# Early-fusion transformer layer: the routing of the last two tiles rewritten, GpSimd's products put ahead of the table loads, a constant's load moved back

## Chip, cores and metric

The kernel runs on one core of a Trainium2 chip. The metric is the device time of one execution in microseconds (us), lower is better. A core has five engines that run on their own and wait for each other by semaphores: TensorE (PE in the profile; PEld is its weight load), VectorE (DVE), ScalarE (ACT), GpSimd (POOL) and SyncE (SP, which only issues transfers), and 16 DMA engines that all queues share.

## What is computed

Eight sequences of 164 tokens (36 patch embeddings and 128 text tokens) with 192 channels pass one attention layer and one mixture-of-experts layer:

```
xn   = layernorm(layernorm(h), ln_w)
attn = causal_softmax((xn * W_qk[h]) (xn * W_qk[h])^T / sqrt(192))      # 12 heads
out  = (attn (xn - mean(wte))) / (position + 1)                         # wte: 50257 x 192
h    = h + out W_o^T
n    = normed(layernorm(h)) * ln_w;  probs = softmax(n W_router)        # 16 experts
keep the first 64 tokens per expert and sequence; y = relu(n wi[e]) wo[e] where kept, else n
h    = h + h_normed + max(probs) * y
```

## The kernel before

**Attention, one sequence at a time** (`iteration(b)` on PE, DVE, ACT and GpSimd, b = 0 to 7; the queues' order is written out by hand). A sequence is cut in 128 rows (A) and 36 rows (B). DVE makes z (the layer-normed rows), PE transposes it, ACT copies it to `zT`. GpSimd multiplies `zT` by the heads' weights `w2` (`weigh`, L385 to 390): six products into `AwA` (three groups of four heads, two halves of the channels each) and two into `AwB`. PE's `score(b, r)` needs them: round r = 0, 1, 2 takes two products of `AwA` each, rounds 3 and 4 take `AwB`. Then DVE takes row maxima (L786, L790), ACT exponentials (L552, L557), DVE the factors `rn` (L798), GpSimd multiplies them in (`normalise`, L416: three tiles of `PA`, two of `PB`). PE transposes P (L1274 to 1280), ACT and DVE copy a high and a low part (`PTAH` L565, `PTAL` L803, `PTB` the same for B), and `value(b, g)` multiplies by the values into `bO` and `bE` (g = 3 is the B part, `PTB0`, `PTB1`); ACT and DVE copy those out (`oTA`, `oTB`, L570, L808), and `project` multiplies by `W_o` into `bJ`, which `residual` adds to `H`. The scores of sequence b + 1 are put between the steps of sequence b. In PE's order `score(b+1, 0)` follows `value(b, 2)`, and `score(b+1, 1)` and `value(b, 3)` come after it.

**The table's mean** runs beside the attention. `wte` comes in 28 chunks of 1344 KB. Two are loaded into `wbuf`'s two slots. 20 are added onto them by transfers that accumulate, issued by GpSimd (`add_wte`, L396 to 401, three in each `iteration` of b = 0 to 5, the slots in turn); each issue waits until the transfer before it in its slot has landed. Six go through one more buffer, `plain` (SP, L284 to 287): DVE sums it in four pieces per sequence (`plain_sum`, L822), and the next load is issued only after the fourth. In DVE's order `plain_sum(b, 0)` stands right in front of `row_max(b + 1, 0)`. During sequence 6 all sums are folded together and the mean is taken out of `H`.

**Routing.** The 1312 tokens lie in 11 tiles (`SLOTS`: eight A tiles, three of 96 B rows). Nine are routed in a first stage (`STAGE[0]`), the last two (A tile of sequence 7, last B tile) in a second. For a stage DVE runs `routed` (maximum, first best expert, one-hot `oh`), PE ranks (`text_rank`: `oh` against constant matrices `mat`), DVE `keep` (`kp`, rank under 64), PE `expert_rank` (counts over all tiles, into `bT`), DVE `place` (row numbers `posI` in the expert table). `row_scales` refines 1/sqrt with one Newton step, `base_factors` makes the factors with which ACT (`bases`) writes the normed rows and the base rows to `pay`. `link` makes DVE wait for each operation before the next. GpSimd then scatters tile after tile to `dispatched` (L458). When all have landed, SP loads the first block of rows, and PE starts the experts with `x_transpose(0, 16)`. From the moment the number of blocks is known until then it runs 34 matmuls on ones (`stay_warm(bJ, 34)`). 16 blocks of 112 rows follow, PE back to back.

`mat` is 1024 KB in float32 (`mat32`), loaded by SP at its queue's start, in front of the first plain load (L304), and copied to bf16 by ACT (L608) between sequences 1 and 2.

Of the kernel before, what the change touches and what calls it, by code (L numbers as in the profile page):

```python
# [58 lines left out]
def program(nc, patches, projw, projb, pos, txtA, txtB, txtBp, wqk, lnw, lnc, wte, wo_attn,  # L59
# [9 lines left out]
    with ctx:  # L69
# [88 lines left out]
        capB = sb("capB", [128, EXP])  # L158
# [122 lines left out]
        def _(sp):  # L281
# [21 lines left out]

            sp.dma_start(mat32, cst2_d[:, C_MAT:NCST2]).then_inc(mat_in, 16)  # L304
            plain_loads(sp)
# [55 lines left out]
        def _(pool):  # L361
# [118 lines left out]
            for j in range(n0, SLOTS):  # L480
                pool.wait_ge(norm_ready, j - n0 + 1)
                pool.wait_ge(base_ready, j + 1)
                scatter(j)
# [26 lines left out]
        def _(act):  # L510
# [94 lines left out]
            iteration(1)  # L605

            act.wait_ge(mat_in, 16)
            nc.scalar.activation(mat[:, :, :].rearrange("p m s -> p (m s)"), mat32, ACT.Copy).then_inc(mat_ready, 1)  # L608
            with act.Fori(2, LAST - 1) as b:
                iteration(b)  # L610

            def bases(g, k0=None, k1=None):
                act.wait_ge(basepar_ready, g + 1)
                lo, hi = GROUPS[g]
                for k in range(lo if k0 is None else k0, hi if k1 is None else k1):
                    if g == 0:
                        nc.scalar.activation(norm[:, k, :], H[:, ORD[k], :], ACT.Identity, bias=nmc[:, k:k + 1],
                                             scale=rsq[:, 1, k:k + 1]).then_inc(cen_ready, 1)
# [14 lines left out]
            def lx_exp(B):  # L633
                k0, k1 = STAGE[B]
                act.wait_ge(le_ready, 2 * B + 2)
                nc.scalar.activation(lx[:, k0:k1, :], lg[:, k0:k1, :], ACT.Exp).then_inc(lx_ready, 1)

# [999 lines left out]
```

## Time and profile before

| | us |
|---|---|
| median of 3 runs (376.38 to 377.46) | 377.38 |
| profiled execution, its own time | 378.11 |
| its span, first to last instruction | 376.3 |
| busy in the span: PE, PEld, DVE, ACT, POOL | 338.9, 308.9, 220.6, 126.1, 169.0 |
| mean granted TensorE clock | 0.962 |

The span divides roughly into set-up (to 25 us), sequences 0 to 7 (to 257), routing (to 291) and experts (to 369). The granted clock is given as a share of the full 2.4 GHz, so 0.50 is 1.2 GHz. Busy shares are means; what counts is which wait ends last at each place.

### The profile page before, as it was taken

Reading aid. Unit: us, or ns where it says so; the run is one execution under the profiler, and the core shown is the slowest. Engines: PE = TensorE matmul, PEld = TensorE weight load, DVE = VectorE, ACT = ScalarE, POOL = GpSimd, SP = SyncE. Lnnn points to the kernel's source line nnn. Section 1 sums busy time; section 2 is a strip of 40 time slices with the busy share of each in tenths; the row PEclk is TensorE's granted clock in tenths of the full one; section 3 lists DMA queues with packets and bytes.
Section 4 is the critical chain, followed back from the end, with each engine's and each line's share of the span. In section 5 each row is a group of like instructions: output and inputs, shape, how many; then the busy total and the mean of one; then the engine's idle time right before and its main releaser. Section 6 shows DMA issues by size and latency. Waiting matters only on the chain.

```text
span 376.3 us, 6812 instructions
## 1 busy us (share of the span) xinstructions
PE 338.9 (90%) x2360; PEld 308.9 (82%) x2360; DVE 220.6 (59%) x556; ACT 126.1 (34%) x433; POOL 169.0 (45%) x181
## 2 busy tenths in 40 slices
PE   5987699999899899899898998998859999999992
PEld 2866499899699799798897998997723999999991
DVE  2378638668669578587677978657485222222221
ACT  2055424644453445426345024539100111111110
POOL 3058474674663862954836203140751134433321
PEclk9699969999999999999999999999968999999997
DMA  7499999799799799898997999600222499999950
GB/s 226 151 410 332 214 207 212 203 194 213 210 200 236 198 188 271 169 195 251 174 210 187 291 209 241 148 0 2 107 95 71 108 288 276 258 250 264 270 150 17
DMA packets 20176, 74.29 MB, mean 197 GB/s; under 512 B 3388, under 2 KB 9021, under 8 KB 18874
## 3 DMA queue, kind: packets, MB, share of 16 engines
q0 software_dynamic: 7344, 30.57, 40.3%
q1 hardware_dynamic: 9898, 40.40, 36.6%
q10 hardware_dynamic: 2912, 3.04, 3.1%
q8 instruction: 12, 0.20, 0.2%
q14 instruction: 10, 0.08, 0.1%
HBM read 66.12 MB, written 9.25 MB: 200 GB/s over the span
## 4 chain that ended last, share of the span: by engine, by line
PE 44%; issue 19%; POOL 15%; DVE 9%; DMA 7%; ACT 4%; POOLq 1%; SPq 0%; DVEq 0%; ACTq 0%
PE bO L1190 19%; PE bE L1190 10%; PE bS L1190 6%; POOL AwA L390 5%; PE bJ L1190 5%; DMA wbuf<-in_wte 4%; POOL PA L416 4%; POOL wbuf L401 3%; POOL AwB L390 2%; DMA AwA<-in_patches 2%; ACT PA L552 2%; PE bT L1190 1%; DVE negmax L786 1%; POOL PB L416 1%; PE bT L1535 1%
## 5 line engine op out<-in xcount | busy, mean ns | idle before, releaser
L552 ACT ACTIVATE PA<-bS,negmax 128x128 f32<-128x128 f32 x96 | 33.9, 366 | 85.4 <-DVE negmax L786 85.4
L416 POOL TENSOR_TENSOR PA<-PA,rn 128x512 f32<-128x512 f32 x24 | 25.5, 1062 | 66.4 <-DVE rn L798 66.3
L390 POOL TENSOR_TENSOR AwA<-zT,w 96x512 f32<-96x512 f32 x45 | 53.4, 1515 | 3.3 <-ACT zT L534 3.3
L1190 PE MATMUL bJ<-wo_sb,oTA 128*128 128x192 f32 x288 | 52.1, 331 | 0.0
L1190 PEld LDWEIGHTS bS<-zT,AwA 96*128 96x128 f32 x384 | 48.4, 198 | 1.2
L1190 PE MATMUL bS<-zT,AwA 96*128 96x128 f32 x384 | 48.4, 281 | 0.0
L1190 PEld LDWEIGHTS bJ<-wo_sb,oTA 128*128 128x128 f32 x288 | 47.2, 193 | 0.0
L1190 PE MATMUL bO<-PA,wx 96*128 96x112 f32 x384 | 45.4, 275 | 0.5 <-DVE PA L1163 0.5
L1190 PEld LDWEIGHTS bO<-PA,wx 96*128 96x128 f32 x384 | 44.9, 192 | 0.7 <-DVE PA L1163 0.7
L463 POOL DMA_INDIRECT out<-PA,yrow x16 | 15.0, 940 | 58.7 <-DVE PA L1179 58.7
L683 ACT ACTIVATE AwA<-bO 128x448 f32<-128x448 f32 x16 | 8.7, 543 | 82.6 <-PE bO L1190 74.1
L1190 PE MATMUL bE<-wx,AwA 128*112 128x192 f32 x192 | 33.8, 326 | 0.0
L822 DVE TENSOR_REDUCE wx<-wx 128x672 f32 (+1 forms) x24 | 31.5, 1314 | 0.0
L1190 PEld LDWEIGHTS bE<-wx,AwA 128*112 128x112 f32 x192 | 30.4, 177 | 0.0
L401 POOL DMA_DIRECT2D wbuf<-in_wte x20 | 27.2, 1359 | 5.0 <-DMA wbuf<-in_wte 3.9
L1172 DVE TENSOR_SCALAR AwA<-bO 128x224 f32<-128x224 f32 x16 | 6.3, 392 | 36.0 <-PE bO L1190 31.8
L786 DVE TENSOR_REDUCE negmax<-bS 128x4 f32<-128x512 f32 x24 | 16.5, 687 | 14.4 <-PE bS L1190 14.3
L416 POOL TENSOR_TENSOR PB<-PB,rn 108x328 f32<-108x328 f32 x16 | 11.7, 733 | 28.1 <-DVE rn L798 27.3
L458 POOL DMA_INDIRECT dispatched<-pay,posI x11 | 12.4, 1125 | 19.3 <-ACT pay L619 13.7
L570 ACT ACTIVATE oTA<-bO,lncol 128x512 f32<-128x512 f32 x24 | 16.6, 690 | 13.1 <-PE bO L1190 13.1
L1190 PE MATMUL bS<-zT,AwB 96*108 96x164 f32 x128 | 20.3, 302 | 0.0
L1190 PE MATMUL bO<-wo_sb,oTB 128*96 128x192 f32 x108 | 18.1, 327 | 2.2 <-DVE oTB L808 1.5
(248 smaller groups left out, 697.2 us busy)
## 6 DMA issues: line engine op xcount, KB each, us to landing
wbuf<-in_wte POOLq DMA_DIRECT2D x20, 1344.0 KB, 12.9
wx<-in_wi SPq DMA_DIRECT2D x16, 576.0 KB
wx<-in_wo SPq DMA_DIRECT2D x16, 576.0 KB
wx<-in_wte SPq DMA_DIRECT2D x6, 1344.0 KB, 8.5
dispatched<-zeros SPq DMA_DIRECT2D x7, 675.5 KB, 10.6
wbuf<-in_wte SPq DMA_DIRECT2D x2, 1344.0 KB, 11.4
AwA<-dispatched ACTq DMA_DIRECT2D x14, 168.9 KB
wo_sb<-in_wo_attn SPq DMA_DIRECT2D x1, 1728.0 KB, 6.7
```

Source lines behind the costliest of these rows:

```text
L390: nc.gpsimd.tensor_tensor(o, zT[:, k, ss].unsqueeze(1).to_broadcast(list(o.shape)), w2[:, k, hs].unsqueeze(2).to_broadcast(list(o.shape)), ...
L401: pool.dma_start(wchunk[s], wv[:, ds(c, 1), :].rearrange("p c x -> p (c x)"), accum_op=ALU.add, max_dma_last_dim=WR * EMB * 4 // 2).then_i ...
L416: nc.gpsimd.tensor_tensor(t, t, q.unsqueeze(2).to_broadcast(list(t.shape)), ALU.mult).then_inc(p_ready, 1)
L458: nc.gpsimd.indirect_dma_start(out=xd[:, :], out_offset=bass.IndirectOffsetOnAxis(ap=posI[0:n, j:j + 1], axis=0), in_=pay[0:n, j, :], in_o ...
L463: nc.gpsimd.indirect_dma_start(out=out[:, :], out_offset=bass.IndirectOffsetOnAxis(ap=idx, axis=0), in_=rows, in_offset=None, bounds_check ...
L552: last = nc.scalar.activation(PA[:, h, :], bank[:, j * SA:(j + 1) * SA], ACT.Exp, bias=negmax[:, h:h + 1], accum_out=lsum[:, h:h + 1])
L570: nc.scalar.activation(dst, src, ACT.Copy, scale=lncol[:, 0:1]).then_inc(o_used, 1)
L683: nc.scalar.activation(hT[:, 0:4, :], bO[0][:, 0:4 * T].rearrange("p (c n) -> p c n", c=4), ACT.Relu).then_inc(h0_ready, 1)
L786: nc.vector.tensor_reduce(negmax[:, 4 * r:4 * r + 4], bS[r % 2][:, :].rearrange("p (h s) -> p h s", h=4), X, ALU.max, negate=True).then_in ...
L822: nc.vector.tensor_reduce(psums.rearrange("p (n e) -> p n e", e=EMB)[:, ds(b, 1), q].rearrange("p n e -> p (n e)"), plain.rearrange("p (r ...
L1172: nc.vector.tensor_scalar(hT[:, 4:6, :], bO[1][:, 0:2 * T].rearrange("p (c n) -> p c n", c=2), 0.0, None, ALU.max).then_inc(h1_ready, 1)
L1190: return nc.tensor.matmul(o, l, r, start=start, stop=stop, skip_group_check=True)
```

## The change

1. GpSimd: in every `iteration`, four `AwA` products stand in front of the first accumulating load instead of behind it, and the other two loads move behind a later step each. In sequence 0 all three `normalise` of `PA` stand in front of the first two loads.
2. SP loads `mat32` behind the six plain loads; ACT copies it to bf16 in sequence 6 instead of between sequences 1 and 2. DVE's factors for sequences 2 to 7 move into sequence 0's iteration, behind its third `e_copy`.
3. Routing: a Newton step has three operations instead of four; `kept` and one of the `drop` operations are gone (`kept` comes once, after the table of blocks); the last two tiles' normed rows come from ACT instead of DVE (L987), their exponents are scaled and summed by ACT (`slot_exp`); stage 0's `row_scales` and `base_factors` move behind `routed`; `shift` spares stage 1 an operation. PE's `expert_rank(0)` stands before `value(LAST, 3)` instead of behind it.
4. `stay_warm(bJ, 34)` becomes `stay_warm(bJ, 26)`.

```diff
-            sp.dma_start(mat32, cst2_d[:, C_MAT:NCST2]).then_inc(mat_in, 16)
             plain_loads(sp)
+            sp.dma_start(mat32, cst2_d[:, C_MAT:NCST2]).then_inc(mat_in, 16)
...
-            normalise(0, range(1))
+            normalise(0, range(3))
             add_wte(2, 0, 0)
-            normalise(0, range(1, 2))
             add_wte(3, 1, 0)
-            normalise(0, range(2, 3))
...
-                for k in range(4):
-                    if r is not None and k < 3:
-                        add_wte_nth(i, r + k)
-                    if k == 0:
-                        weigh(b + 1, t_before(b, "z") + 1, (0, 1), (0, 1))
-                    elif k == 1:
-                        weigh(b + 1, t_before(b, "z") + 1, (0, 1), (2,))
-                        normalise(b + 1, (0,))
-                    elif k == 2:
-                        normalise(b + 1, (1,))
-                        weigh(b + 1, t_before(b, "z") + 1, (0, 1), (3,))
-                    else:
-                        normalise(b + 1, (2,))
+                n = t_before(b, "z") + 1
+                weigh(b + 1, n, (0, 1), (0, 1))
+                if r is not None:
+                    add_wte_nth(i, r)
+                weigh(b + 1, n, (0, 1), (2,))
+                normalise(b + 1, (0,))
+                if r is not None:
+                    add_wte_nth(i, r + 1)
+                normalise(b + 1, (1,))
+                weigh(b + 1, n, (0, 1), (3,))
+                if r is not None:
+                    add_wte_nth(i, r + 2)
+                normalise(b + 1, (2,))
...
+            def slot_exp(k):
+                act.wait_ge(le_ready, 3)
+                act.wait_ge(basepar_ready, 1 + k - GROUPS[0][1] + 1)
+                nc.scalar.activation(lx[:, k, :], lg[:, k, :], ACT.Exp, scale=rsq[:, 1, k:k + 1],
+                                     accum_out=lsm[:, k:k + 1]).then_inc(lx_ready, 1)
...
-                link(nc.vector.tensor_tensor(t, t, x, ALU.mult))
-                link(nc.vector.tensor_scalar(t, t, -0.5, 1.5, ALU.mult, ALU.add))
-                link(nc.vector.tensor_tensor(y, y, t, ALU.mult))
+                link(nc.vector.scalar_tensor_tensor(t, t, -0.5, x, ALU.mult, ALU.mult))
+                link(nc.vector.scalar_tensor_tensor(y, t, 1.5, y, ALU.add, ALU.mult))
...
             row_factor(0, 2)
-            factors(2, NBATCH, 2)
...
                 e_copy(b, 2)
+                if is0(b):
+                    factors(2, NBATCH, 2)
                 plain_sum(b, 0)
...
-            row_scales(0)
-            base_factors(0)
...
             routed(0)
-            exponents(0)
+            row_scales(0)
+            exponents()
+            base_factors(0)
             keep(0)
-            probability(0)
+            homes(0)
             place(0)
...
             routed(1)
-            norms(2)
-            exponents(1)
+            row_scales(2)
             keep(1)
-            probability(1)
+            base_factors(2)
+            homes(1)
             place(1)
...
-            value(LAST, 3)
+            project(LAST, 12, 14)
             pe.wait_ge(t_used, TPB * NBATCH)
             pe.wait_ge(tl_used, 5 * NBATCH)
             expert_rank(0)
-            project(LAST, 12, WCH)
+            value(LAST, 3)
+            project(LAST, 14, WCH)
...
-            stay_warm(bJ, 34)
+            stay_warm(bJ, 26)
```

GpSimd, the loop's body for an even sequence, before (`wbuf<-in_wte` is an accumulating load, ISA rows are register and semaphore work):

```order
L416 TENSOR_TENSOR PB<-PB,rn 108x328
L399 ISA
L401 ISA
L401 DMA wbuf<-in_wte 128x2x1344
L385 ISA
L390 TENSOR_TENSOR AwA<-zT,w 96x512 x4
L401 ISA
L401 DMA wbuf<-in_wte 128x2x1344
L390 TENSOR_TENSOR AwA<-zT,w 96x512 x2
```

The same place of the changed kernel:

```order
L416 TENSOR_TENSOR PB<-PB,rn 108x328
L385 ISA
L390 TENSOR_TENSOR AwA<-zT,w 96x512 x4
L399 ISA
L401 ISA
L401 DMA wbuf<-in_wte 128x2x1344
L390 TENSOR_TENSOR AwA<-zT,w 96x512 x2
```

The four products no longer stand behind a load, and the second load has moved on behind `normalise(b + 1, 0)`, which is not shown; the third moved from ahead of `normalise(b + 1, 1)` to behind the two `AwB` products.

DVE in the second stage of the routing, from the one-hot to the placing's first operation, before:

```order
L1008 TENSOR_TENSOR oh<-cst,lidx 128x32
L724 TENSOR_TENSOR nwt<-rsq 128x2
L725 TENSOR_TENSOR nwt<-nwt,var 128x2
L726 TENSOR_SCALAR nwt<-nwt 128x2
L727 TENSOR_TENSOR rsq<-rsq,nwt 128x2
L978 TENSOR_SCALAR rsq<-rsq 128x1
L979 SCALAR_TENSOR_TENSOR nmb<-fmv,rsq 128x1
L987 TENSOR_SCALAR pay<-H,fmv,rsq 128x192
L1012 TENSOR_TENSOR lg<-lg,rsq 128x32
L1024 SCALAR_TENSOR_TENSOR kp<-bS,oh 128x32
L1027 TENSOR_REDUCE kept<-kp 128x2
L1028 TENSOR_SCALAR drop<-kept 128x2
```

And of the changed kernel:

```order
L1001 TENSOR_TENSOR oh<-cst,lidx 128x32
L726 TENSOR_TENSOR nwt<-rsq 128x2
L727 SCALAR_TENSOR_TENSOR nwt<-nwt,var 128x2
L728 SCALAR_TENSOR_TENSOR rsq<-nwt,rsq 128x2
L1024 SCALAR_TENSOR_TENSOR kp<-bS,oh 128x32
L978 SCALAR_TENSOR_TENSOR nmc<-fmv,rsq 128x1
L979 TENSOR_SCALAR rsq<-rsq 128x1
L980 SCALAR_TENSOR_TENSOR nmb<-fmv,rsq 128x1
L1018 TENSOR_SCALAR drop<-lidx 128x2
L1036 TENSOR_SCALAR capI<-bT 128x16
```

`kp`, which PE waits for, now follows the Newton step directly, and four operations instead of nine lie between it and the placing (before, three more followed the last row shown: `drop`, `lsm` and the reciprocal).

## Rows read from the trace of the kernel before

**Rows 1.** Timeline of PE, sequence 0: start, length, instruction [idle before <-releaser].

```profile
38.14 0.31 PE L1233 MATMUL bT<-cst,zA 128*96 128x128 f32 x1 [2.03 <-DVE PTAL L803]
...
47.58 0.59 PE L1190 MATMUL bS<-maskA,idb 128*128 128x512 bf16 x1 [2.94 <-issue]
...
56.59 0.44 PE L1190 MATMUL bO<-PTB0H,vAH 128*128 128x432 f32 x1
```

**Rows 2.** Timeline of POOL, sequence 0.

```profile
44.21 1.21 POOL L401 DMA_DIRECT2D wbuf<-in_wte  x1 [2.11 <-DMA wbuf<-in_wte]
44.97 4.49 POOL L390 TENSOR_TENSOR AwA<-zT,w 96x512 f32<-96x512 f32 x4
```

**Rows 3.** Windows: busy of PE, PEld, DVE, ACT, POOL, PEclk, DMA share, GB/s.

```profile
48.00:50.00 2.00, 2.00 (x11) 2.00 (x10) 0.00 (x0) 0.00 (x0) 1.46 (x2) 0.50 1.03 210
...
98.00:124.00 26.00, 24.27 (x175) 22.91 (x174) 19.06 (x37) 11.73 (x47) 15.91 (x16) 1.00 0.93 207
```

**Rows 4.** Timeline of DVE, sequence 0.

```profile
44.67 0.48 DVE L808 TENSOR_SCALAR oTA<-bE,lncol 128x256 f32<-128x256 f32 x1 [1.44 <-PE bE L1190]
...
51.62 0.69 DVE L786 TENSOR_REDUCE negmax<-bS 128x4 f32<-128x512 f32 x1 [5.26 <-PE bS L1190]
```

**Rows 5.** Timeline of PE, sequence 3.

```profile
102.17 0.39 PE L1190 MATMUL bS<-maskA,idb 128*128 128x512 bf16 x1 [0.92 <-POOL AwA L390]
...
108.67 0.43 PE L1190 MATMUL bO<-PTB0H,vAH 128*128 128x432 f32 x1 [0.26 <-DVE PTB1L L803]
```

**Rows 6.** Timeline of POOL, sequence 3, and the products of sequence 6.

```profile
98.76 1.21 POOL L401 DMA_DIRECT2D wbuf<-in_wte  x1
...
109.42 1.21 POOL L401 DMA_DIRECT2D wbuf<-in_wte  x1 [0.28 <-issue]
...
203.46 6.03 POOL L390 TENSOR_TENSOR AwA<-zT,w 96x512 f32<-96x512 f32 x6
```

**Rows 7.** Who waited, 60 to 200 us: total, times, longest.

```profile
PE bS L1190 <- POOL AwA L390: 4.1, 5, 0.9
...
PE bT L1233 <- DVE PTAL L803: 0.4, 1, 0.4
```

**Rows 8.** Timeline of DVE, sequences 3 and 4.

```profile
104.38 0.69 DVE L786 TENSOR_REDUCE negmax<-bS 128x4 f32<-128x512 f32 x1 [1.39 <-PE bS L1190]
...
127.94 1.31 DVE L822 TENSOR_REDUCE wx<-wx 128x672 f32 x1
```

**Rows 9.** The plain loads' line L287, 100 to 180 us: issue starts, landing.

```profile
L287 SPq DMA_DIRECT2D wx<-in_wte x3: 328/328/328, 118.2 to 170.6; - x3
...
DMA to landing us min/median/max: 8.0/8.5/8.8
```

**Rows 10.** DMA queues, 146 to 148 us: packets, MB, share of 16 engines.

```profile
q0 software_dynamic: 70, 0.33, 81.1%
q1 hardware_dynamic: 17, 0.18, 21.9%
```

**Rows 11.** Timelines of DVE and PE, first stage of routing.

```profile
259.88 0.17 DVE L1039 TENSOR_SCALAR capI<-bT 128x16 int32<-128x16 f32 x1 [1.41 <-PE bT L1190]
...
263.39 3.14 PE L1190 MATMUL bO<-wo_sb,oTB 128*96 128x192 f32 x18 [1.51 <-DVE oTB L808]
```

**Rows 12.** Timeline of DVE, second stage.

```profile
272.68 0.19 DVE L1008 TENSOR_TENSOR oh<-cst,lidx 128x32 bf16<-128x32 f32 x1
...
274.43 0.18 DVE L1024 SCALAR_TENSOR_TENSOR kp<-bS,oh 128x32 bf16<-128x32 f32 x1
...
278.87 0.16 DVE L1062 TENSOR_TENSOR posI<-drop,posF 128x2 int32<-128x2 f32 x1
```

**Rows 13.** Timelines of PE and SP before the experts.

```profile
281.15 9.88 PE L1190 MATMUL bJ<-ones 128*128 128x512 bf16 x34 [1.49 <-DVE nbI L1147]
...
285.21 1.27 SPq L238 DMA_DIRECT2D AwA<-dispatched  x3
```

**Rows 14.** Window at that place, columns as in rows 3.

```profile
288.00:289.00 1.00, 1.00 (x7) 0.46 (x5) 0.00 (x0) 0.00 (x0) 0.00 (x0) 1.00 0.17 60
```

More of the change, by code:

```diff
@@ L604, in _ @@
             iteration(0)
[L605 to L609, printed above, removed]
+            with act.Fori(1, LAST - 1) as b:
                 iteration(b)
@@ L646, in _ @@
             o_copy(b, 2)
+            act.wait_ge(mat_in, 16)
+            nc.scalar.activation(mat[:, :, :].rearrange("p m s -> p (m s)"), mat32, ACT.Copy).then_inc(mat_ready, 1)
             exps(LAST, (0,))
@@ L676, in _ @@
             nt_slot(7, 10, bO[1])
-            lx_exp(1)
+            slot_exp(9)
+            slot_exp(10)
             bases(2)
@@ L1008, in routed, with exponents, homes @@
                 nc.vector.tensor_tensor(part(oh, B), em, part(lidx, B).unsqueeze(2).to_broadcast(bc), ALU.is_equal).then_inc(oh_ready, 1)
-            def exponents(B):
-                (k0, k1), s = STAGE[B], STAGE[B][1] - STAGE[B][0]
-                nc.vector.tensor_tensor(part(lg, B), part(lg, B), rsq[:, 1, k0:k1].unsqueeze(2).to_broadcast([128, s, EXP]),
+            def exponents():
+                (k0, k1), s = STAGE[0], STAGE[0][1] - STAGE[0][0]
+                nc.vector.tensor_tensor(part(lg, 0), part(lg, 0), rsq[:, 1, k0:k1].unsqueeze(2).to_broadcast([128, s, EXP]),
                                         ALU.mult).then_inc(le_ready, 1)
             def probability(B):
-                dve.wait_ge(lx_ready, B + 1)
-                link(nc.vector.tensor_reduce(part(lsm, B), part(lx, B), X, ALU.add))
+                if B:
+                    dve.wait_ge(lx_ready, 3)
+                else:
+                    dve.wait_ge(lx_ready, 1)
+                    link(nc.vector.tensor_reduce(part(lsm, B), part(lx, B), X, ALU.add))
                 nc.vector.reciprocal(pay[:, STAGE[B][0]:STAGE[B][1], D_RP], part(lsm, B)).then_inc(rp_ready, 1)
+            def homes(B):
+                link(nc.vector.tensor_scalar(part(drop, B), part(lidx, B), float(T), float(BIG + EXP * T), ALU.mult, ALU.add))
             def keep(B):
@@ L1026, in keep @@
                 dve.wait_ge(kp_ready, B + 1)
-                link(nc.vector.tensor_reduce(part(kept, B), part(kp, B), X, ALU.add))
-                link(nc.vector.tensor_scalar(part(drop, B), part(kept, B), -float(BIG), float(BIG + EXP * T), ALU.mult, ALU.add))
-                link(nc.vector.scalar_tensor_tensor(part(drop, B), part(lidx, B), float(T), part(drop, B), ALU.mult, ALU.add))
             def place(B):
@@ L1059, in place @@
                     link(nc.vector.tensor_tensor(u, u, t, ALU.add))
-                link(nc.vector.tensor_tensor(u, u, part(kp, B), ALU.mult))
+                link(nc.vector.scalar_tensor_tensor(u, u, -float(BIG), part(kp, B), ALU.add, ALU.mult))
                 link(nc.vector.tensor_reduce(part(posF, B), u, X, ALU.add))
+                probability(B)
                 nc.vector.tensor_tensor(part(posI, B), part(drop, B), part(posF, B), ALU.add).then_inc(pos_ready, 1)
+                if not B:
+                    link(nc.vector.scalar_tensor_tensor(shift[:, :], cst2[:, C_EM:C_EM + EXP], -float(T), first[:, 0, :],
+                                                        ALU.mult, ALU.subtract))
             b = NBATCH - 2
```

45 lines of the change are left out of this document (20 added, 25 removed).

## Prediction

> **What bounds the kernel now.** I read the page's slices of busy time first, then the windows, then the list of waits, and then each engine's timeline at the places that the diff touches. In the middle sequences PE is busy 24.3 of 26 us at full clock [rows 3]. So PE's order is the bound, and only its idle pieces can be won. The list of waits between 60 and 200 us has one large one, for `AwA` from GpSimd: 4.1 us in five waits of up to 0.9 [rows 7], one per sequence, in front of `score(b+1, 0)` [rows 5]. Three places differ from this pattern. In sequence 0 PE stands 2.03 us for DVE's low part, then 2.94 us in front of `score(1, 0)` [rows 1], and then runs at half clock, 0.50 in the window at 48 us [rows 3]. In the routing a chain of small DVE operations bounds [rows 11, 12]. Before the experts PE runs matmuls whose results nobody reads [rows 13]. The experts themselves the change leaves alone. The DMA engines are the second resource to watch: their share is 0.93 between 98 and 124 us [rows 3].
>
> **Sequence 0.** (a) DVE's six linked operations for sequences 2 to 7 leave the place in front of the low parts. The wait for these is 2.03 us [rows 1]. Six operations at about 0.2 us, one of them stretched, make 1.9 us; I take 1.85, bounds 1.2 (six at 0.2) and 2.03 (the whole wait). All that follows shifts with it. (b) In front of `score(1, 0)` GpSimd waits 2.11 us for a landed load, issues one in 0.76 us (44.21 to 44.97) and only then starts the products [rows 2], while PE waits 2.94 [rows 1]. After the change the products come directly behind `normalise`, and the load's wait falls behind them. The products start then at about 40.8 us: the first two `wte` issues, now between the `PA` and `PB` tiles, cost some 0.5 of what was open. Two products take 2.0 us (six take 6.03 when no load stands among them [rows 6]), so the score starts at 42.9 instead of 47.58: 4.7 us with (a) in it. (c) The clock. From `score(1, 0)` to `value(0, 3)` the trace has 9.0 us at sequence 0 [rows 1] and 6.5 at sequence 3 [rows 5]. The difference, 2.5 us, is the half clock behind the stall. With the stall reduced to some 0.4 us I expect no drop. (d) Back comes 0.55 us: the moved factors, now five operations of 0.2, and `plain_sum(0, 0)` of 1.3 us [rows 8] stand between DVE's third copy, which ends at 45.1 [rows 4] and then at 43.25, and `row_max(1, 0)`, which starts then at 45.65 instead of 45.1. Together 4.7 + 2.5 - 0.55 = **6.65 us**, bounds 4.0 (the clock falls all the same) and 7.2.
>
> The price of this part lies on the DMA side: the first accumulating load is issued at 36.5 us, behind three `normalise`, instead of at 31.6. Each of those loads occupies the engines for 6.5 us (1344 KB at 210 GB/s [rows 3]). I followed the slots forward: GpSimd then sits behind a landing until about 59.0 us, in front of `normalise(1, 2)`, which PE wants 2 us later. I count nothing for it, up to 2 us in the range.
>
> **The loop, b = 1 to 5.** With the products in front of the load, the first two are done 2.0 us after the last `PB` tile, while PE has `value(b, 2)` to do for 2.5. So the 0.82 us mean wait falls, 4.1 us in all [rows 7]. But the loads move: the three issues, now at 0, 4.8 and 10.7 us after the last `PB` tile [rows 6], would come at 4.1 (four products), 9.7 (two more and a `normalise`) and 15.9 us (another and `AwB`). Their transfers, three times 7 us, then end at 27 us instead of 23. The plain load issued 19.5 us after that tile, at 118.2 [rows 9], now finds 5.6 us of accumulating traffic in front of it or beside it; before, it found 1. Its `plain_sum` comes 9.7 us after the issue, at 127.94 [rows 8], and it lands after 8.0 to 8.8 us [rows 9]. If both queues share the engines evenly, the plain load takes 3.3 + 3.3 us of engine time instead of 3.3 + 1.0, and lands 2.3 us later, after 10.8: 1.0 us too late. The sum stands in DVE's order directly ahead of `row_max(b+1, 0)`, which has 1.39 us of slack [rows 8], of which the earlier score takes 0.92 [rows 5]. So about 0.5 us of delay reaches `exps`, the `PTB` copies and `value(b, 3)`, which waits for these already [rows 5]. Net 0.9 - 0.5 = 0.4 us a sequence, **2.0 us**. The bounds: +4.1 if the plain load is in time, and -9.9 if it is served only when no accumulating packet is there (a landing after 13.1 us, 2.8 us of delay a sequence: 4.1 - 14).
>
> What speaks for even sharing: while the one drained and the other came, the queues had 81% and 22% of the engines in a window of 2 us [rows 10], and the window's tail, in which the plain queue has the larger part, cannot be told from draining. The Trainium skill says the same as my assumption with an open side: by "DMA: Bandwidth & Descriptors", section "Queues, rings and completion order", each engine goes round the queues and changes only at the end of a packet, which may hold many descriptors. By that rule the plain load can be kept from half of the engines' time at least, and more where the accumulating packets are the longer ones; no run here shows it yet.
>
> The constants' copy on ACT (between sequences 1 and 2) held up P's transposed tiles: PE waited 0.4 us once [rows 7]. It moves to sequence 6, where ACT stands idle for over 15 us while DVE folds the table. **0.4 us**. The transfer, 1024 KB, leaves the crowded start, which helps the first loads, and comes behind the sixth plain load; it is wanted 30 us later.
>
> **Routing, first stage.** PE now does `expert_rank(0)` before `value(LAST, 3)`. In the trace `place(0)` began at 259.88 after a wait of 1.41 us, and PE stood 1.51 us for `oTB`, the copy behind it [rows 11]. The ranks were done at 256.7; `kp` follows 0.35 later, two chunks of `project` fill that, the counts take 0.7, so `place` starts at about 258.0. It and the probability that moved into it (0.55) end 1.3 us earlier. The copy then waits for PE's `value` (ends 260.5) less than for DVE; `project_b` starts at 262.25 instead of 263.39. **1.1 us**. Below is nothing if DVE's nine operations between one-hot and `kp` do not fit into PE's last `project` (they need 1.4 us, PE gives 1.5); above is the whole wait, 1.5. ACT's eighteen rows start 2.2 us later and end at 265.1, before GpSimd needs any of them.
>
> **Second stage.** From the one-hot to `posI` the trace has 272.68 to 279.03, 6.35 us [rows 12], all of it linked DVE work. What goes: one Newton operation 0.2, the normed row on DVE 0.45, the scaling 0.1, `kept` 0.22, one `drop` 0.2, the sum of exponents 0.22, one `first` 0.2; what comes is 0.1 for a factor. **1.4 us**, bounds 1.1 and 1.6. ACT's two exponents with sums (not in the trace in this size; nearest the 128x32 one, 0.23, and the attention's 0.37 with 0.19 for the read of the sum) and its rows end 2 us before they are waited for.
>
> **The filler.** 34 matmuls take 9.88 us [rows 13]: about twelve at half clock (0.43) and 22 at full (0.214). The eight that go are of the fast kind: 1.7 us. What is late next is the first block of rows: SP issues its loads at 285.21 [rows 13], and the transfers are over in the window from 288 to 289 [rows 14]. Landed at 288.5 to 289, against a filler that would end at 289.3, they just fit. **1.7 us**, below 1.2.
>
> **Sum.** 6.65 + 2.0 + 0.4 + 1.1 + 1.4 + 1.7 = 13.25 us. Against the profiled execution's own 378.11 (1.8 over its span) that is 364.9; the median of the three runs lies 0.7 below that execution, at 377.38, so **364.1 us**.
>
> **Rivals.** Less than 0.3% (1.1 us) either way cannot be told from no change.
> - *The plain load is in time.* The accumulating tail gives way, as the plain queue's larger share at the end of that window might mean. The loop gives all its 4.1 us: 362.0. Chance 0.22.
> - *The plain load is served last* (the packet rule at its hard end). `plain_sum` holds `row_max` by 1.2 to 2.8 us a sequence: 367.5 to 375.6. Chance 0.15.
> - *GpSimd's late first loads catch up with it in sequence 1, or the clock falls in sequence 0 all the same.* 2 to 2.6 us are lost: 366.5. For it speaks that the DMA engines have only 7% of air; against it, that the slots come round every two loads. Chance 0.12.
> - *Slower.* The same place in DVE's order as the second, but with the plain load also delayed by the next sequence's accumulating load: then the delay is no longer bounded by 2.8 us. The gains outside the loop are 11.25, the loop's own 4.1, so from 3.1 us of delay a sequence the kernel is slower; at 3.6 it is 380. Against it: the next accumulating load is issued only 10 us after the plain one. Chance 0.03.
> - *My forecast*: 0.48, its own range 362.8 to 366.
>
> Faster by over 0.3%: 0.95; within: 0.02; slower: 0.03. The range holds the forecast, the first rival and the third, and the mild half of the second: 360.8 to 368.8.
>
> **What the profile would show.** No idle for POOL `AwA` in front of `score(b+1, 0)`, sequence 0 included, and PEclk 1.0 from 46 to 54 us. `value(0, 3)` near 50 us. The distance of sequences 25.7 us instead of 26.15 (25.3 if the plain load is in time), with DVE waiting on a DMA at L822 if I am right. `posI` of the last tiles 4.9 us after the one-hot, and PE's filler ending about when the rows land. A distance of 26.5 or more, or half clock again in sequence 0, would make the prediction wrong.

## Result and profile after

The changed kernel takes **373.29 us** (median of 4 runs, 372.15 to 373.82); the kernel before, run beside it, takes 376.94 (4 runs, 376.38 to 377.46). The ratio is 0.9889, with a 95% interval of 0.985 to 0.9929. It is 3.65 us faster, where I forecast 13.25: 364.1 us, range 360.8 to 368.8. The measured time lies 4.5 us above the upper end of the range. The profiled execution took 373.52 us, with a span of 371.8. A few kernels below have one execution in a slower state of the chip: the ratios leave it out, the medians do not, and it moves none of them by more than 0.7 us.

Sequence 0 first. PE's timeline of the changed kernel (start, length, instruction, idle time and its releaser):

```profile
40.08 0.39 PE L1195 MATMUL bE<-PTAH,vAH 128*128 128x256 f32 x1 [0.94 <-DVE oTA L809]
...
51.00 0.43 PE L1195 MATMUL bO<-PTB0H,vAH 128*128 128x432 f32 x1 [2.22 <-DVE PTB1L L804]
```

Two windows of the same trace (stretch, its length, busy time and count of PE, PEclk, DMA share, GB/s) answer to [rows 3]:

```profile
44.00:48.00 4.00, 4.00 (x35) 1.00 1.05 215
...
80.00:84.00 4.00, 4.00 (x18) 0.50 1.04 207
```

The waits of 2.03 and 2.94 us [rows 1] are gone, the clock is full from 44 us on, and `value(0, 3)` starts at 51.00 instead of 56.59: 5.6 us won. One new wait stands there, 2.22 us for DVE's low part. The second window is sequence 1: half clock, which the kernel before has only in sequence 0.

Who waited from 60 to 200 us in the changed kernel (total, times, longest), against [rows 7]:

```profile
DVE wx L823 <- DMA wx<-in_wte: 9.6, 5, 2.3
PE bO L1195 <- DVE PTB1L L804: 9.3, 5, 2.2
```

The wait for `AwA` has gone from the list, as it should. In its place `plain_sum` waits for its load in every sequence, and PE for the low part behind it. The chain that ended last shows how one hangs on the other (start, length, what):

```profile
116.71 10.98 DMA wx<-in_wte
128.29 0.81 issue
129.10 0.70 DVE negmax L787
130.09 1.24 ACT PA L550 x7
131.32 0.43 ACT PTB0H L563
131.78 0.61 DVE PTB0L L804
132.67 0.57 DVE PTB1L L804
133.38 1.43 PE bO L1195 x6
```

(Pieces between these lines are left out.) The plain load is now a link of the chain in each of sequences 1 to 5 (15% of the whole span). The line of its issues says "10.8/11.3/12.0" us from issue to landing, against 8.0/8.5/8.8 [rows 9]. VectorE at that place, against [rows 8]:

```profile
127.84 1.35 DVE L823 TENSOR_REDUCE wx<-wx 128x672 f32 x1 [1.29 <-DMA wx<-in_wte]
129.10 0.68 DVE L787 TENSOR_REDUCE negmax<-bS 128x4 f32<-128x512 f32 x1
```

The 1.3 us of idle time in front of `row_max` have become idle time in front of the sum, and `row_max` starts late. While both queues are at work, 124 to 126 us, they share the engines' time evenly (packets, MB, share of 16 engines):

```profile
q1 hardware_dynamic: 40, 0.43, 52.2%
q0 software_dynamic: 38, 0.20, 50.0%
```

Following PE from sequence to sequence: `value(b, 3)` is 5.6 us ahead of before in sequence 0, 3.8 in 1, 1.7 in 2, 1.4 in 3, 0.5 in 4 and 0.7 us behind in sequence 5. From sequence 1 to 5 the distance of sequences is 27.5 us on average, where I forecast 25.7, named 26.5 as the sign of being wrong, and the kernel before has 26.3. By the end of the loop nothing of the start is left. Behind it the routing wins back. DVE's timeline there, against [rows 11, 12]:

```profile
258.75 0.18 DVE L1036 TENSOR_SCALAR capI<-bT 128x16 int32<-128x16 f32 x1 [0.74 <-PE bT L1195]
...
272.18 0.19 DVE L1001 TENSOR_TENSOR oh<-cst,lidx 128x32 bf16<-128x32 f32 x1
...
277.04 0.14 DVE L1062 TENSOR_TENSOR posI<-drop,posF 128x2 int32<-128x2 f32 x1
```

And PE's, against [rows 11, 13]:

```profile
262.88 3.14 PE L1195 MATMUL bO<-wo_sb,oTB 128*96 128x192 f32 x18 [0.34 <-DVE oTB L809]
...
279.28 7.24 PE L1195 MATMUL bJ<-ones 128*128 128x512 bf16 x26 [1.51 <-DVE nbI L1151]
```

From the one-hot to `posI` it is 5.0 us instead of 6.35, and the filler takes 7.24 instead of 9.88. The first expert's matmuls start at 287.20 instead of 291.70, although PE came out of the loop 0.9 us later than before.

### The profile page after: what moved, and what is told of

It is laid out like the page before. It is cut to its first block, busy times and chain, and to the rows that moved or that the text cites. A ratio compares the mean times of both kernels' runs of the same rounds, so it can differ in the third digit from the quotient of the medians.

```text
span 371.8 us, 6815 instructions
## 1 busy us (share of the span) xinstructions
PE 334.1 (90%) x2352; PEld 307.1 (83%) x2352; DVE 221.0 (59%) x546; ACT 127.0 (34%) x438; POOL 167.9 (45%) x181
## 4 chain that ended last, share of the span: by engine, by line
PE 47%; DVE 19%; DMA 18%; ACT 7%; issue 6%; DVEq 1%; POOLq 0%; SPq 0%; ACTq 0%
PE bO L1195 22%; DMA wx<-in_wte 15%; PE bE L1195 13%; PE bS L1195 5%; PE bJ L1195 4%; ACT PA L550 3%; DVE negmax L787 3%; DMA AwA<-in_patches 2%; DVE wx L823 2%; DVE vBL L814 2%; DVE vAL L816 1%; DVE vBL L816 1%; PE bT L1195 1%; DVE PTB0L L804 1%; DVE PTB1L L804 1%
## 5 line engine op out<-in xcount | busy, mean ns | idle before, releaser
L416 POOL TENSOR_TENSOR PA<-PA,rn 128x512 f32<-128x512 f32 x24 | 25.4, 1059 | 70.1 <-DVE rn L799 69.9
L390 POOL TENSOR_TENSOR AwA<-zT,w 96x512 f32<-96x512 f32 x45 | 48.1, 1157 | 3.3 <-ACT zT L532 3.3
L1195 PEld LDWEIGHTS bS<-zT,AwA 96*128 96x128 f32 x384 | 46.7, 192 | 1.1
L1195 PE MATMUL bS<-zT,AwA 96*128 96x128 f32 x384 | 46.8, 275 | 0.0
L401 POOL DMA_DIRECT2D wbuf<-in_wte x20 | 24.2, 1234 | 8.4 <-DMA wbuf<-in_wte 5.6
L550 ACT ACTIVATION_READ_ACCUMULATOR PA<-bS,negmax 128x1 f32 x96 | 19.5, 203 | 0.0
L809 DVE TENSOR_SCALAR oTA<-bE,lncol 128x256 f32<-128x256 f32 x24 | 11.5, 477 | 13.3 <-PE bE L1195 13.3
## 6 DMA issues: line engine op xcount, KB each, us to landing
wx<-in_wte SPq DMA_DIRECT2D x6, 1344.0 KB, 11.5
```

The lines of the kernel that those rows point to most:

```text
L390: nc.gpsimd.tensor_tensor(o, zT[:, k, ss].unsqueeze(1).to_broadcast(list(o.shape)), w2[:, k, hs].unsqueeze(2).to_broadcast(list(o.shape)), ...
L401: pool.dma_start(wchunk[s], wv[:, ds(c, 1), :].rearrange("p c x -> p (c x)"), accum_op=ALU.add, max_dma_last_dim=WR * EMB * 4 // 2).then_i ...
L416: nc.gpsimd.tensor_tensor(t, t, q.unsqueeze(2).to_broadcast(list(t.shape)), ALU.mult).then_inc(p_ready, 1)
L550: last = nc.scalar.activation(PA[:, h, :], bank[:, j * SA:(j + 1) * SA], ACT.Exp, bias=negmax[:, h:h + 1], accum_out=lsum[:, h:h + 1])
L809: nc.vector.tensor_scalar(dst, src, lncol[:, 1:2], None, ALU.mult).then_inc(e_used, 1)
L1195: return nc.tensor.matmul(o, l, r, start=start, stop=stop, skip_group_check=True)
```

## Experiments

My theory after the result: the accumulating loads that the products-first order moves run beside the plain load; it lands 1.3 to 2.3 us too late; and because its sum stands ahead of `row_max(b+1, 0)`, PE pays. Rivals: the DMA engines' throughput bounds the loop whatever the order; the late first loads are at fault; the order costs something other than the plain load. Seventeen kernels followed. All ratios are to the kernel before on the same chip (376.5 to 377.0 us). Each is uncertain by 0.25 to 0.46%, so a difference between two of these kernels is uncertain by some 2 us.

**1. GpSimd's old order in the loop.** From sequence 1 on:

```diff
-weigh(b + 1, n, (0, 1), (0, 1)); add_wte_nth(i, r)
+add_wte_nth(i, r); weigh(b + 1, n, (0, 1), (0, 1))   # r+1, r+2 likewise
```

> The changed kernel, but from sequence 1 on GpSimd issues each accumulating load in front of the products again, as before the change; sequence 0 keeps the new order. Theory (the moved accumulating loads run beside the plain load, which lands 1.9 us too late per sequence, and PE pays for it): plain_sum has no wait on a DMA, the wait for AwA is back at 0.9 us, the loop keeps the distance of 26.15 us, and the 5.6 us of the start and the 5.4 us of routing and filler both arrive: span 365.5, time 367. Rival A (the DMA engines' throughput is the bound of the loop, so that a start won on PE is given back whatever the order): the plain load is still waited for, distance about 27 in sequences 1 to 3, time 371 to 374. Rival B (half clock in sequence 1 comes with the later first loads): 2.8 us of it stay, time 370.

Measured: **372.55 us** (0.988, 0.9844 to 0.9916). From sequence 2 on it is as the theory says: no wait for the plain load, `AwA` back at 0.9. Sequence 1 is not. GpSimd's timeline:

```profile
76.89 1.21 POOL L401 DMA_DIRECT2D wbuf<-in_wte  x1 [3.98 <-DMA wbuf<-in_wte]
77.65 2.50 POOL L390 TENSOR_TENSOR AwA<-zT,w 96x512 f32<-96x512 f32 x2
```

And VectorE's, in front of the low part for which PE waits:

```profile
78.46 1.73 DVE L818 TENSOR_SCALAR rn<-rinv,cst 128x4 f32<-128x4 f32 x1
```

The plain load is 3.07 us late. The late pair of products then holds a scaling that takes 0.23 us elsewhere until its own end (80.19 and 80.15 us; run 11 takes this up). Together they give PE a wait of 3.54 us, and a granted clock of 0.65 from 80 to 84 us. So what the start had won was lost around sequence 1, where transfers had piled up; the time alone would have looked like rival A, and rival B's half clock is part of it.

**2. Only two products in front of the first load.**

```diff
-weigh(b + 1, n, (0, 1), (0, 1)); add_wte_nth(i, r)
+weigh(b + 1, n, (0, 1), (0,)); add_wte_nth(i, r); weigh(b + 1, n, (0, 1), (1,))   # r+1, r+2 where they were before the change
```

> As the run before, but from sequence 1 on the first accumulating load stands behind two of the six products (not none, not four), the second and third as before the change. Theory: only one transfer moves, by 2.0 us, and it is the one farthest from the plain load: the wait for AwA is gone and plain_sum waits under 0.5 us a sequence: distance 25.5 to 25.9, time 363 to 366. Rival A (throughput of the DMA engines): 371 to 374, like the changed kernel. Rival C (the load two places later waits for this one's slot, GpSimd then comes late with a normalise): waits of GpSimd on wbuf over 1 us a sequence and PE waiting for AwA or PA; 367 to 370.

Measured: **370.76 us** (0.9824, 0.9778 to 0.987), at the edge of rival C and not in the theory's range. The plain load waited only in sequences 1 and 2 (2.39, 1.03), but GpSimd waited for its slots eight times, 21.7 us in all, up to 5.1.

**3. One swap in VectorE.**

```diff
-plain_sum(b, 0); row_max(b + 1, 0)
+row_max(b + 1, 0); plain_sum(b, 0)
```

> The changed kernel with one swap in VectorE's order: row_max(b+1, 0) ahead of plain_sum(b, 0), so that the late plain load no longer stands in front of the maximum. Theory: the exponents start 1.3 to 2.6 us earlier, the delay now stands in front of the low part PTB0 and is 1.3 us shorter there: PE's wait at value(b, 3) falls from 1.9 to about 0.6 us, 5 to 6 us in all, time 367 to 368.5. Rival A (throughput of the DMA engines is the bound): the wait only moves, 372 to 374.

Measured: **365.84 us** (0.9705, 0.967 to 0.974), 7.4 us from one swapped pair, 1.2 us more than the theory's range allows. PE's wait at `value(b, 3)` fell to 0.64 us as forecast, and sequence 1 has no half clock any more (1.00 from 76 to 84 us), which the theory had not counted. The plain load lands as late as before (11.5 us on the page), but VectorE never waits for it. VectorE's timeline of this run in one of the middle sequences:

```profile
123.88 0.69 DVE L787 TENSOR_REDUCE negmax<-bS 128x4 f32<-128x512 f32 x1 [1.53 <-PE bS L1195]
124.49 2.55 DVE L823 TENSOR_REDUCE wx<-wx 128x672 f32 x2
```

The distance of sequences is 25.7 us. So a late load costs what stands behind its wait. Rival A, the DMA engines' throughput as the bound, is out: the same transfers run, and the time falls.

**4. Half a plain load.**

```diff
-sp.dma_start(plain, wv[:, c, :])
+sp.dma_start(plain[:, 0:WR * EMB // 2], wv[:, c, 0:WR * EMB // 2])   # loads 2 to 6
```

(Shortened; c stands for the chunk's number.) This kernel leaves out half of five chunks, so it does not compute the table's mean.

> The changed kernel with plain loads 2 to 6 cut to their first half (672 KB instead of 1344; the sums then take old rows for the other half, so the table's mean is not computed). Theory and rival A both have the wait for the plain load gone: 9.6 us of waits on VectorE and 9.3 on PE fall, the distance is 25.3, time 362 to 365, and the half clock in sequence 1 goes with the stall that came before it. Rival D (the products-first order costs something besides the plain load, such as the second normalise coming late): the distance stays at 26.4 or more, time 370 or more.

Measured: **365.02 us** (0.9678, 0.9639 to 0.9717). The waits for the plain load fall from 9.6 us to 2.6, and the distance of sequences to 25.4 to 26.1 us from sequence 1 on, under rival D's 26.4: it is out as the main cost.

**5. The swap in the kernel before.**

> The kernel before, with the one swap alone: row_max(b+1, 0) ahead of plain_sum(b, 0). In its trace plain_sum never waits on a DMA, and row_max waits for PE's score by 1.28 to 1.39 us as it is. Theory (the swap is worth what the plain load's lateness costs, and the kernel before has none): no change, 375.5 to 377.5. Rival (the order in VectorE is worth 7 us by itself, in any kernel): 369 to 371.

The edit is that of run 3, on the kernel before. Measured: **378.46 us** (1.0038, 1.0012 to 1.0063): slightly slower, where equal was expected. The swap wins nothing in a kernel whose plain load is in time; it costs about 1.5 us. The trace says where: the sum now stands in front of the low part, and PE's wait at `value(b, 3)` is 0.64 us a sequence instead of 0.26.

**6. The change without GpSimd's part**: order of GpSimd and place of the factors as before; routing, constants and filler as changed.

> The changed kernel with GpSimd's order and the place of the factors of sequences 2 to 7 as before: what is left of the change is the routing, the later constants and the filler of 26. Theory: start and loop as before, routing and filler 5.4 us from the traces, 0.4 for the constants' copy: 370.7 to 372.5, so less time than the whole change (372.9 to 373.3), whose GpSimd part then is worth nothing or costs up to 2 us. Rival (part of what the two traces differ by behind the loop belongs to the earlier loads): 373.5 or more.

Measured: **369.04 us** (0.9802, 0.9771 to 0.9833), below every case, and 4.2 us faster than the whole change (3.3 by the ratios). So GpSimd's part (with the factors' place), from which I forecast most of the gain, costs 3 to 4 us.

**7. The constants' load and copy alone.** ACT's copy moves to sequence 6 as well, which the cut does not show.

```diff
-sp.dma_start(mat32, cst2_d[:, C_MAT:NCST2]).then_inc(mat_in, 16)
 plain_loads(sp)
+sp.dma_start(mat32, cst2_d[:, C_MAT:NCST2]).then_inc(mat_in, 16)
```

> The kernel before with one thing of the change alone: the 1024 KB of routing matrices are loaded behind the sixth plain load instead of in front of the first, and ACT's copy of them moves to sequence 6. I priced it at 0.4 us. Theory now: the load held back the first accumulating loads for which GpSimd waits in sequence 0; without it GpSimd's 2.1 us wait falls, the score of sequence 1 comes earlier and the half clock behind the stall goes: 4 us less, 372 to 373.5. Rival (as predicted): 376.0 to 376.5, and what the run without GpSimd's part gained (7.7 us) is all routing and filler.

Measured: **373.34 us** (0.9909, 0.9877 to 0.9941): 3.2 us from the term that I had at 0.4. GpSimd issues its third load at 42.29 us instead of 44.21 [rows 2], PE waits 1.39 instead of 2.94 us in front of `score(1, 0)`, the clock stays full, and `value(0, 3)` starts at 52.62. The 4.3 us from here to run 6 (4.0 by the ratios) are routing and filler.

**8. The products-first order alone** (run 6 plus that order in the loop).

> The changed kernel with its first two loads and the factors of sequences 2 to 7 both at their places of before: against the run without GpSimd's part (369.04 us) it differs by the products-first order alone. Theory (the order moves the loads beside the plain load; plain_sum waits 1.3 to 2.1 us in each of sequences 1 to 5, PE the same, against 0.9 for AwA won): 0.6 to 1 us lost a sequence, 3 to 5 us, 372 to 374. My prediction's step has it as 2 us won: 367. Rival (the 4 us that the whole GpSimd part costs are all in the start, the factors held by GpSimd's products): 368 to 369.5.

Measured: **374.29 us** (0.9916, 0.9877 to 0.9956), 5.3 us slower than run 6 (4.3 by the ratios), where my step had 2.0 faster. It is 0.3 us above the theory's range. VectorE's waits for the plain load are 8.5 us in five, but not alike as the theory had them: 3.17, 0.18, 2.62, 0.40 and 2.17 us. PE waits 3.12 us in sequence 1, and the granted clock is 0.79 from 76 to 84 us.

**9. The first two loads put back** in the changed kernel.

```diff
-normalise(0, range(3)); add_wte(2, 0, 0); add_wte(3, 1, 0)
+normalise(0, (0,)); add_wte(2, 0, 0); normalise(0, (1,)); add_wte(3, 1, 0); normalise(0, (2,))
```

> The changed kernel with nothing but its first two accumulating loads put back between GpSimd's three normalisations (31 us instead of 36). Theory A (in the changed kernel the loop's loss has two parts: the moved loads of the loop, 1.3 to 2.1 us a sequence from sequence 2 on, and the late start, whose backlog makes the 2.2 us stall and the half clock of sequence 1): sequence 1 comes without half clock, the later waits of plain_sum stay, 369 to 371. Theory B (the late start carries on into all sequences, the loop's order costs nothing): the waits of plain_sum are gone, 364 to 366. Theory C (the late start has no part): 372.5 to 374.

Measured: **376.47 us** (0.9994, 0.9968 to 1.002), outside all three theories. `plain_sum` waits 1.6 to 2.2 us in every sequence as before, so the late start is not what delays it. Sequence 1 is without half clock (1.00 from 80 to 84 us), as theory A has it. What I had not seen is in sequence 0. VectorE's timeline of this run:

```profile
42.69 1.04 DVE L728 TENSOR_TENSOR nwz<-rstd 128x12 f32<-128x12 f32 x1
43.76 3.16 DVE L729 SCALAR_TENSOR_TENSOR nwz<-nwz,nmr 128x12 f32<-128x12 f32 x1
46.96 0.17 DVE L730 SCALAR_TENSOR_TENSOR rstd<-nwz,rstd 128x12 f32<-128x12 f32 x1
```

GpSimd's at the same time:

```profile
39.67 4.04 POOL L390 TENSOR_TENSOR AwA<-zT,w 96x512 f32<-96x512 f32 x4
43.65 1.17 POOL L401 DMA_DIRECT2D wbuf<-in_wte  x1
44.41 2.47 POOL L390 TENSOR_TENSOR AwA<-zT,w 96x512 f32<-96x512 f32 x2
```

Two of the moved factors, 0.17 us of work each, end at 43.73 and 46.92 us, when GpSimd's products end (43.71, 46.88). PE waits 4.73 us for what follows, and the granted clock is then 0.59 from 53 to 57 us. In the changed kernel GpSimd happens to wait for a slot just there (2.61 us), and the same operation takes 0.96.

**10. The factors put back** in the changed kernel.

> The changed kernel with the factors of sequences 2 to 7 back in front of the low parts of sequence 0. I priced their move at 1.85 - 0.55 = 1.3 us won. In the traces their five operations in the new place are held by GpSimd's products by 0.8 to 3.2 us. Theory: the move is worth under 1 us where GpSimd waits for its load just then (the changed kernel): 372.5 to 374.5. Rival (as priced): 374.5 or more. If the time is under 372.5 the new place costs more than the old.

Measured: **373.78 us** (0.992, 0.9886 to 0.9954). The move is worth 0.5 us by the medians and 1.2 by the ratios, both less than they can tell, so the times neither show nor refute its price of 1.3. In the trace `value(0, 3)` starts at 50.25 us; with the factors moved it starts between 50.22 and 51.00 (the changed kernel and runs 1, 2 and 4, the same up to there). So in sequence 0, where I had looked for the gain, there is none to be seen.

**11. Carrying the swap on.** Three steps on the changed kernel. First, VectorE does maxima and low parts ahead of sums and factors:

```diff
-if is0(b): factors(2, NBATCH, 2)
-plain_sum(b, 0); row_max(b + 1, 0); plain_sum(b, 1); t_low(b, 3)
-row_factor(b + 1, 0); t_low(b, 4); row_max(b + 1, 1); plain_sum(b, 2)
+row_max(b + 1, 0); plain_sum(b, 0); t_low(b, 3); row_factor(b + 1, 0); t_low(b, 4)
+row_max(b + 1, 1)
+if is0(b): factors(2, NBATCH, 2)
+plain_sum(b, 1); plain_sum(b, 2)
```

> The run with the sum behind the maximum, carried on: VectorE does row_max(b+1, 0), plain_sum 0, both low parts, row_max(b+1, 1) and only then plain_sum 1 and 2; in sequence 0 the moved factors also stand behind row_max(1, 1). Theory: the waits at value(b, 3) that were left there, 1.96 us in sequence 0 and 0.64 in each later one, were VectorE's own work in front of PTB1's low part: they fall, and so does the low clock behind the wait in sequence 0 (about 1 us): 365.8 - 2 - 1 - 3.5 = 359.5, at most 362. Rival (the DMA engines' throughput now ends last, 26 loads of 6.5 us from 36 us on): the plain load is waited for again, in front of plain_sum or at slot_total, 364 to 366.

Measured: **361.87 us** (0.96, 0.9567 to 0.9634). PE's waits of 0.64 us in the loop fell to 0.26, and the clock behind sequence 0 is full (1.00 from 50 to 58 us). The wait in sequence 0 did not fall: PE still waits 2.17 us there. VectorE's timeline:

```profile
47.66 2.14 DVE L799 TENSOR_SCALAR rn<-rinv,cst 128x4 f32<-128x4 f32 x1
49.72 0.59 DVE L804 TENSOR_TENSOR PTB1L<-bT,PTB1H 36x432 fp32r<-36x432 f32 x1
```

GpSimd's pair of products in this run starts at 47.27 and lasts 2.49: to 49.76. The 128x4 scaling was held until then. Second, the scaling behind the low part:

```diff
-row_factor(b + 1, 0); t_low(b, 4)
+t_low(b, 4); row_factor(b + 1, 0)
```

> The run with maxima and low parts first (361.87 us), with row_factor(b+1, 0) behind the second low part instead of between the two. There in sequence 0 the 128x4 scaling of row_factor took 2.14 us instead of 0.23 and ended with GpSimd's products, and PE waited 2.17 us behind it. Theory (VectorE's operations from SBUF to SBUF are held while GpSimd works, the low part, which reads PSUM, is not): PE's wait in sequence 0 falls under 0.4 us and the 0.26 us of each later sequence goes: 358.5 to 360. Rival (any VectorE operation is held by GpSimd there, so the low part is held instead): the same wait, 361 to 362.5.

Measured: **359.12 us** (0.954, 0.9506 to 0.9574). VectorE's timeline at that place:

```profile
47.88 0.59 DVE L804 TENSOR_TENSOR PTB1L<-bT,PTB1H 36x432 fp32r<-36x432 f32 x1
48.39 0.16 DVE L797 RECIPROCAL rinv<-lsum 128x4 f32<-128x4 f32 x1
48.59 1.59 DVE L799 TENSOR_SCALAR rn<-rinv,cst 128x4 f32<-128x4 f32 x1
```

And GpSimd's:

```profile
47.65 2.50 POOL L390 TENSOR_TENSOR AwA<-zT,w 96x512 f32<-96x512 f32 x2
```

The low part, which reads PSUM, takes its 0.59 us in the midst of the products; the scaling is held to their end. The reciprocal between them is not held, though it too goes from SBUF to SBUF: the theory as written is too wide. PE waits for neither. Third, GpSimd's first two loads early again, as in run 9:

> The run before this one, with GpSimd's first two loads between its three normalisations again, as before the change, so 5 us earlier. Theory (the backlog of the DMA engines after the start is what makes GpSimd wait for its slots in sequences 0 and 1, up to 2.6 us each): those waits fall; the normalisations come later, which PE pays with 0.5 to 1 us at the start. Net within 1 us of the run before, 358 to 360.5. Rival (the start's normalisations are worth more): 361 or more.

Measured: **358.86 us** (0.9516, 0.9473 to 0.956), the same as the step before. GpSimd's waits for slots in sequence 0 are gone, and PE has gained nothing by it. The distance of sequences is 24.6 us.

**12. The second step, with GpSimd's old loop order.**

> The run with the low part ahead of the factor, but from sequence 1 on GpSimd issues its loads in front of the products, as before the change. It prices the products-first order where VectorE no longer puts the plain load's sum in front of the maximum. Theory: the wait for AwA is back at 0.9 us a sequence, five times, and sequence 1 is without a stall: 4 to 5 us more than that run, 363 to 365. Rival (the new VectorE order needs only the plain load to be early, the products' order is worth nothing): within 1 us of that run.

Measured: **368.62 us** (0.9773, 0.9739 to 0.9807), 9.5 us more (8.8 by the ratios), above both cases. About 4 are the loop's from sequence 2 on (distances of 25.6 to 25.9 us instead of 24.6 to 24.8), 5.9 are sequence 1's: GpSimd waits 2.46 us for a slot in front of the products, PE 3.32 for them, and the clock is 0.70 from 68 to 76. With VectorE's order right, the products-first order is worth about 1 us a sequence, more than the 0.4 that I had forecast. Sequence 1's part belongs to the old order together with late first loads, as in run 1: run 6, with the old order and early loads, has no such stall. With VectorE's new order that pair was not tried.

**13. The filler.** 34 on run 3, then 34 and 18 on the third step of run 11.

> The run with the sum behind the maximum (365.84 us), with 34 matmuls without a reader instead of 26. My prediction priced the eight at 1.7 us (all at full clock): 367.5. Theory from the trace after, where 26 took 7.24 us against 9.88 for 34: 2.6 us, 368.4. Rival (what ends last there is the rows' transfer, not the filler): no change, 365.8.

> The run with early loads and VectorE's new order (358.86 us), with 34 matmuls without a reader instead of 26. In the traces of the pair before, the eight made 1.4 us, while the medians differed by 0.3. If PE's filler is what the first expert's matmuls wait for: 360.3 to 361.5. If the rows' transfer ends last: 358.9.

> The same with 18. By my prediction's step the rows land about when 26 end, so eight fewer give nothing, or half clock in the experts costs something: 358.5 to 361. If the filler still ends last at 26: 357.2.

Measured: **366.13** against 365.84 us; **359.34** and **358.31** against 358.86. In the traces eight matmuls make 1.4 us in the first pair and 1.65 in the second (8.55 us for 26, 10.20 for 34). The medians have 0.3 to 0.6 us, less than they can tell, so the times do not show that fewer matmuls gain anything; all three pairs only point the same way. With 18, PE waits for the rows, as its timeline shows:

```profile
271.76 0.40 PE L1543 MATMUL bT<-cst,AwA 112*96 112x112 f32 x2 [0.71 <-DMA AwA<-dispatched]
```

The fastest kernels are these: 358.3 us with 18 (0.9498, 0.9458 to 0.9537) and 358.9 with 26, 5% below the kernel before; a difference between the two is not shown.

## Why the prediction was wrong, step by step

- **Sequence 0, 6.65 us forecast, 5.6 in the trace.** Size about right, cause mostly wrong. The constants' load, which I noted as a help to "the first loads" and gave no time, brings 4.0 us of it by itself (run 7: 52.62 against 56.59, half clock gone). The products ahead of the load add 0.8 (run 8: 51.83), and the three normalisations ahead of the first two loads about as much again or more (50.22 to 51.00). These are single traces, and traces of kernels that are the same up to there differ by up to 0.8 us. Step (d) priced the moved factors at 0.2 us each and looked only at VectorE's order. Beside GpSimd's products one of them takes 0.96 to 3.16 us, and nothing of term (a) less (d) is to be seen in sequence 0 (run 10).
- **The loop, +2.0 us forecast, -5.3 measured (run 8; -4.3 by the ratios). This is the step that failed.** In the traces of the changed kernel and the one before, 6.5 us are lost between `value(0, 3)` and `value(6, 3)`. The mechanism was right: waits for `AwA` gone, loads moved beside the plain load, even sharing of the engines, the sum in front of `row_max`. Its sizes were each a little off, all to one side. The plain load lands after 11.3 us (10.8 to 12.0), not 10.8, since accumulating traffic is beside it to its very end. The sum then starts 1.3 to 2.3 us late, 1.9 on average (9.6 in five), not 1.0. And of the slack 0.3 us took up delay, not 0.5: PE's wait at `value(b, 3)` went from 0.26 us [rows 5] to 1.86 (9.3 in five). Where I let 0.5 us reach PE it is 1.6, against 0.8 won at `AwA`: 0.8 lost a sequence, 4 us in five. The step subtracted numbers of nearly the same size, and 0.9 us more lateness with 0.2 us less slack turned its sign. Sequence 1 adds half clock behind the stall, which I had looked for in sequence 0 only. That the plain load's wait in front of `row_max` is what costs is shown by runs 3 and 4. (The 5.6 us of traffic that the step names do not follow from its own ends, 27 less 19.5; the sum does not use them.)
- **The rival "served last" had the outcome (1.2 to 2.8 us, 367.5 to 375.6) for a reason that the traces refute.** (By the prediction's own terms its range is 368.0 to 376.0.) By the Trainium skill, "DMA: Bandwidth & Descriptors", section "Queues, rings and completion order", an engine goes round the queues and changes at the end of a packet. I took this for a possible bias against the plain load; the window shows 40 packets and 52.2% for it, 38 and 50.0% for the accumulating queue. I gave that outcome 0.15 since I had tied it to unfair sharing.
- **The rival on late first loads** was half right: put back, they take away sequence 1's half clock (run 9), but not the waits of `plain_sum`, and the time is no better (376.47 us).
- **Constants' copy, 0.4 us forecast:** 3.2 with its load (run 7). The copy's own part is about what I forecast: from `value(1, 3)` to `value(2, 3)` run 7 has 26.25 us instead of 26.82.
- **Routing 1.1 + 1.4 and filler 1.7, together 4.2 us: 4.3 measured** (run 6 against run 7, 4.0 by the ratios). The traces have more, 5.4 us: the second stage gave 1.35 (the terms that I listed for it add up to 1.5, not 1.4), the first 1.4 and the filler 2.6. The times cannot tell 4.3 from 5.4. The filler's 9.88 to 7.24 us is 1 us more than eight matmuls at full clock, since fewer of those left ran at half clock; 1.4 to 1.65 in pairs with like clocks.

## What to carry to other kernels

A wait for a transfer costs what stands behind it in the engine's order: put the operations that feed the bottleneck ahead of it, and the same late load costs little (7.4 us won here, from one swapped pair; where the load is in time, the swap cost 1.5 us). Price a crowded DMA stretch by what leaves it as well as by what enters it; a megabyte that nobody needs before the routing cost 3.2 us at the start. When two edits move transfers, measure each alone: here a gain of 3 us, one of 4 and a loss of 3 to 4 looked like one small gain.

## What the runs showed of the hardware

- **Some operations of VectorE are held by GpSimd.** Products of two 128x12 operands in SBUF and a 128x4 scaling (0.17 to 0.23 us alone) took 0.96 to 3.16 us beside GpSimd's products. The five held rows shown here end within 0.04 us of GpSimd's end. Low parts, which read one operand from PSUM, kept their 0.59 us. Not all that stays in SBUF is held: a reciprocal of 128x4 took 0.16 us (run 11), and a sum of `plain` its usual time beside four products (kernel before, [rows 2]):

```profile
45.08 1.28 DVE L822 TENSOR_REDUCE wx<-wx 128x48 f32<-128x672 f32 x1
```

  The Trainium skill, "SBUF — State Buffer", section "SBUF: two separate sides", says that an instruction of GpSimd and one of VectorE that runs in a two-port mode, or has two SBUF inputs (this against one of GpSimd that reads SBUF), lock a shared port pair against each other for the whole instruction. The traces agree for the products: in the changed kernel, beside a run of four products of 1.0 us each, two factors ended at 43.47 and 44.47 us, at the ends of the third and the fourth. Behind a DMA issue, though, VectorE was held over both products of a pair (2.14 us in run 11), and in run 9 over the issue too. Why is open.
- **An accumulating load takes the engines about twice as long per byte as a plain one.** In the window from 124 to 126 us, 0.20 MB took 50.0% of the engines' time and 0.43 MB took 52.2%. From 98 to 124 us in the same kernel it is 3.92 MB in 78.5% against 1.20 MB in 11.3%, which is 5.2 against 2.4 us per MB.
- **The granted clock falls behind some stalls of PE and not behind others of the same length.** After 2.22 us at 51.0 us it stayed at 1.00 (the changed kernel). After 2.21 us at 78.08 it was 0.50 (the same kernel), after 1.82 at 80.56 it stayed at 1.00 (run 9), after 1.96 at 50.85 it was 0.73 from 52 to 56 (run 3). The same stall of the same program can go either way: 2.27 us at 50.93 left 0.53 from 50 to 54 in run 4, which is the changed kernel up to there. What decides is open. As an estimate, each fall costs 1 to 3 us: the missing 0.27 over 4 us is 1.1 (run 3), the missing 0.50 over 6 us is 3.0 (the changed kernel, 78 to 84 us).
